# Perceiver layers on one core: in both cross attentions three of four rounds of scores stand later in their half sequence, and the last value projection stands between the turns of tiles 11 and 12

## What is computed

```
def _L1_xattn_ref(query, key, value, mask, Wq, bq, Wk, bk, Wv, bv, Wo, bo):
    q = _split_heads(query @ Wq.T + bq)
    k = _split_heads(key @ Wk.T + bk)
    v = _split_heads(value @ Wv.T + bv)
    scores = jnp.einsum('bhqd,bhkd->bhqk', q, k) / jnp.sqrt(jnp.float32(DEPTH))
    scores = scores + mask * jnp.float32(-1000000000.0)
    weights = jax.nn.softmax(scores, axis=-1)
    ctx = jnp.einsum('bhqk,bhkd->bhqd', weights, v)
    ctx = ctx.transpose(0, 2, 1, 3).reshape(query.shape[0], -1, D_MODEL)
    return ctx @ Wo.T + bo
```

## Time and profile before

| | us |
|---|---|
| median of 3 runs | 2361.56 |
| lowest and highest run | 2360.01, 2362.49 |
| the profiled execution | 2358.21 |
| its span | 2356.4 |
| busy in the span: PE, PE weight loads | 2071.3, 1579.9 |
| busy in the span: DVE, ACT, POOL | 1347.8, 1091.2, 474.8 |

### The profile page before, as it was taken

How to read it: one execution, slowest core, us unless ns; L and a number is a source line. 1 busy time by engine, 2 the same in 40 slices (tenths; PEclk the granted TensorE clock), 3 DMA queues, 4 the chain that set the end, 5 groups by cost and what they waited for, 6 DMA issues and landing times. The chain is left out here.

```text
span 2356.4 us, 60046 instructions
## 1 busy us (share of the span) xinstructions
PE 2071.3 (88%) x25136; PEld 1579.9 (67%) x25136; DVE 1347.8 (57%) x3549; ACT 1091.2 (46%) x2087; POOL 474.8 (20%) x377
## 2 busy tenths in 40 slices
PE   6899999999999985567996899999999999997874
PEld 3677777777777762346994677777777777764453
DVE  4466666666666657834114466666666666663685
ACT  1644545554454543511321455554555554451681
POOL 2311112221111100211002333332223333200010
PEclk9999999999999997787998999999999999996857
DMA  2111111111111001032321311121211112100000
GB/s 87 40 47 30 30 30 30 39 33 45 30 30 30 17 2 54 1 107 99 115 100 47 83 44 53 45 61 44 58 44 44 53 46 61 30 2 21 1 1 25
DMA packets 62413, 103.60 MB, mean 44 GB/s; under 512 B 15417, under 2 KB 30914, under 8 KB 62146
## 3 DMA queue, kind: packets, MB, share of 16 engines
q1 hardware_dynamic: 62146, 99.76, 14.4%
HBM read 98.70 MB, written 1.05 MB: 42 GB/s over the span
## 5 line engine op out<-in xcount | busy, mean ns | idle before, releaser
L628 DVE CUSTOM_DVE_ANT_0 maps_d<-scores_d,mask_scaled_d 128x512 f32<-128x512 f32 (+1 forms) x512 | 263.6, 572 | 212.3 <-PE scores_d L491 205.1
L628 DVE CUSTOM_DVE_ANT_0 maps_a<-scores_a,no_mask_a 128x512 f32<-128x512 f32 (+1 forms) x512 | 263.6, 572 | 208.7 <-PE scores_a L491 208.7
L501 PE MATMUL turn_a<-const,maps_a 128*128 128x128 f32 (+1 forms) x1664 | 259.3, 282 | 21.3 <-DVE mapsT_a L656 15.4
L501 PE MATMUL turn_d<-const,maps_d 128*128 128x128 f32 (+1 forms) x1664 | 259.3, 282 | 21.3 <-DVE mapsT_d L656 15.3
L501 PEld LDWEIGHTS turn_d<-const,maps_d 128*128 128x128 f32 (+1 forms) x1664 | 184.3, 142 | 79.2 <-issue 30.2
L501 PEld LDWEIGHTS turn_a<-const,maps_a 128*128 128x128 f32 (+1 forms) x1664 | 184.2, 142 | 79.2 <-issue 30.2
L580 ACT ACTIVATE mapsT_a<-turn_a 128x512 f32<-128x512 f32 x224 | 129.7, 595 | 230.6 <-PE turn_a L501 230.5
L580 ACT ACTIVATE mapsT_d<-turn_d 128x512 f32<-128x512 f32 x224 | 129.7, 595 | 230.4 <-PE turn_d L501 230.3
L585 ACT ACTIVATE maps_a<-maps_a,neg_max_a 128x1024 f32<-128x1024 f32 (+1 forms) x256 | 222.0, 952 | 1.9 <-DVE neg_max_a L635 1.9
L585 ACT ACTIVATE maps_d<-maps_d,neg_max_d 128x1024 f32<-128x1024 f32 (+1 forms) x256 | 222.0, 952 | 1.9 <-DVE neg_max_d L635 1.9
L284 POOL CAST ctx_hi_a<-raw_a 128x1024 fp32r<-128x1024 f32 x64 | 55.0, 860 | 585.0 <-PE project_a L110 451.1
(11 more groups left out here) (395 smaller groups left out, 4409.0 us busy)
## 6 DMA issues: line engine op xcount, KB each, us to landing
raw_a<-in_ctxT SPq DMA_DIRECT2D x48, 512.0 KB, 3.9
raw_d<-in_ctxT SPq DMA_DIRECT2D x48, 512.0 KB, 3.9
w_c<-in_L_ffn_W SPq DMA_DIRECT2D x23, 1024.0 KB, 5.3
mask_scaled_d<-in_mask SPq DMA_DIRECT2D x32, 400.2 KB, 5.2
raw_a<-in_ctxT SPq DMA_DIRECT2D x16, 65.0 KB, 2.0
raw_d<-in_ctxT SPq DMA_DIRECT2D x16, 65.0 KB, 2.0
x<-in_x SPq DMA_DIRECT2D x1, 1024.0 KB, 5.8
Wk_c_b<-in_L_attn_Wk_c SPq DMA_DIRECT2D x1, 1024.0 KB, 7.0
```

The source lines that it names most:

```text
L501: ins = nc.tensor.transpose(TP[at % 2][0:r, P * j:P * j + P], maps[g % 2][:, j, P * t:P * t + r], chip.ident)
L628: nc.vector.tensor_tensor_reduce(maps[b][:, j, cols], SC[j][:, 0:w], mf[m % 2][:, cols] if masked else none[:, 0:w], 1.0, NEG, ALU.add, AL ...
```

## The change

The second and third round move behind other work of their own tile, the fourth moves from tile 6 to tile 7, and the last value unit of a half sequence moves from tile 12 (even) or tile 9 (odd) to tile 11. In the PE loop, a round at tile 2 (`ROUND_LAST`) now comes behind the values of tiles 0 and 1, and a round at a tile that also has a key unit (tiles 4 and 7) now comes behind that unit. DVE's and ACT's code is as it was; their order follows the tables.

```diff
-V_AT = [{3: 0, 6: 1, 9: 2, 12: 3}, {3: 4, 6: 5, 9: 6}]
-ROUND_AT = {0: 0, 2: 1, 4: 2, 6: 3}
+V_AT = [{3: 0, 6: 1, 9: 2, 11: 3}, {3: 4, 6: 5, 11: 6}]
+ROUND_AT = {0: 0, 2: 1, 4: 2, 7: 3}
+ROUND_LAST = (2,)
...
                     turn(g, t)
-                    if t in ROUND_AT and g + 1 < GROUPS:
+                    if t in ROUND_AT and t not in ROUND_LAST and t not in K_AT and g + 1 < GROUPS:
                         scores(g + 1, ROUND_AT[t])
                     if t in K_AT and m + 1 < NB:
                         k_unit(m + 1, 4 * h + K_AT[t])
+                    if t in ROUND_AT and t in K_AT and g + 1 < GROUPS:
+                        scores(g + 1, ROUND_AT[t])
                     if t in V_AT[h] and m + 1 < NB:
                         v_unit(m + 1, V_AT[h][t])
...
                         values(g, t - 2)
                         values(g, t - 1)
+                    if t in ROUND_LAST and g + 1 < GROUPS:
+                        scores(g + 1, ROUND_AT[t])
```

## The result

The changed kernel takes **2415.38 us** (median of 4 runs, 2413.70 to 2420.52) against 2360.78 us (4 runs) for the kernel before: a ratio of 1.0236 [1.0217, 1.0255], or 54.6 us slower. The forecast was 2427 us in a range of 2396 to 2455, from a sum of +65. The profiled execution was the slowest of the four, 2420.52 us with a span of 2418.7.

The account below looks back on a forecast made before the run. PE's list sets the time, through its waits and order. Odd half sequences 1.00 and even ones 1.29 slower give 66.2, with -1 for the ends +65; from 2358.2 profiled to 2423.4, plus 3.4 for the median: 2427 us, range 2396 to 2455.

Parts of the forecast that it names:

- Up to tile 3: Second round of scores starts at 4.65 without the 0.43 wait; tile 3 starts 0.52 earlier.
- Tile 4: k1 must wait for v0's keep on ACT and starts at 8.58, losing 0.53.
- rival of a quick keep: The keep ahead of k1 is quicker than taken, so no loss there: 31 us less, 2396; 6%.
- Tiles 4 to 9: PE is 0.10 ahead at tile 9; DVE's `negate` comes at 18.11 instead of 14.18; ACT's `exp` still costs nothing.
- The value unit stands in the backlog: At tile 11 the last value unit waits 1.34 us for k3's keep, behind DVE's `finish` and move of tile 10.
- the value unit fills the wait: Rival: k3's keep is done by 21.86, the unit starts at once, saving 38 us: 2324; 6%.
- The odd half sequence: An odd half sequence takes 25.82 us, 1.00 slower than 24.82; 15 per attention.
- the move of tile 10 1.96 later: On DVE, the move of tile 10 starts 1.96 after `finish`, at 22.17, with k3's keep following at 22.77 to 23.05.
- the end after the turn of tile 12: In odd half sequences the turn of tile 12 starts at 23.98, its values at 25.46, the next half sequence at 25.82.
- the even half sequence: v3 starts at 24.54 and no longer covers tile 12's move; the half sequence is 1.29 slower than 26.65.
- The clock: No fall expected from waits of 1.34 and 1.0 us; the rival of a fall adds 51 us, 2478; 6%.
- The last but one half sequence: It has no projections and waits for DVE's rounds; the later fourth round was to gain about 1.3 us.

Follow-up runs that it names:

- Experiment 8: The kernel before with only the second round moved behind the values of tiles 0 and 1: 2351.83 us, 0.9958.
- Experiment 3: The changed kernel with the values of tiles 2 and 3 put ahead of k1 at tile 4: 2387.79 us, 1.0112.
- Experiment 2: The kernel before with only the last value unit moved to tile 11: 2402.64 us, 1.0176.
- experiment 10: `order_only` with `finish` split (tiles 8 and 2), values ahead of k3, last value unit at tile 11: 2311.52 us; without that unit's move 2275.32.
- Experiment 4: The changed kernel with the sums and DVE's `finish` at tile 12 instead of 9: 2399.85 us, 1.0162.
- `order_only`: The kernel before with second and fourth rounds behind their tile's values, and at tile 4 values, k1, then third round: 2317.46 us, 0.9808.

## Why the prediction was right, and where it was off

- **What bounds the kernel.** Right: PE's list and its waits. The stretches of the two attentions grew by 55.1 us, with PE's busy time by 15.0.
- **Up to tile 3.** Right: the second round started at 4.66 without idle (forecast 4.65). Experiment 8 shows its worth alone, 10.7 us.
- **Tile 4.** k1 started at 8.59 (forecast 8.58), with 0.34 idle in the record. From start to start that is a loss of 0.53, just what was forecast. The 0.15 from the end of a keep to the next product, for which the prediction shows no row, measured 0.14 here (425.93 to 426.07) and 0.15 at tile 11. Experiment 3 prices this wait: 27.6 us, where the rival of a quick keep had 31. That rival did not happen.
- **Tiles 4 to 9.** The turn of tile 9 started at 18.38 (forecast 18.45), `negate` at 18.05 (18.11), the reciprocal at 20.12 (20.21). `exp` cost nothing, as forecast, with 0.98 of cover where 1.3 was forecast.
- **The value unit stands in the backlog.** Right as to what ends its wait: in the odd half sequence k3's keep ended at 22.86 and not by 21.86, with DVE busy all the way from `negate`, so the rival ("the value unit fills the wait") fell. The wait was 1.17 from start to start (440.49 less 438.91 less 0.41) where 1.34 was forecast; the record shows 0.93 of it as idle, where "about 1.3" was to be seen, and 0.66 in even half sequences where 1.0 was. Experiment 2 gives the unit's place 41 of the 55 us. Too narrow is the thought that it is all the backlog: experiment 10 has the same place cost 36 us without one.
- **The size was high by 10 us in the sum** (65 against 54.6; the forecast of 2427 was 11.6 above the measured time). The odd half sequence was 0.34 shorter than forecast. The term that was mis-sized is the step "the move of tile 10 1.96 later": it measured 1.86 (437.60 to 439.46). The 1.96 held a last instruction of `finish` of 0.37, beside which POOL was at work (0.44 us from 426.06); in the changed kernel, where POOL does that work later, it is 0.28 in all 64 half sequences. With 0.09 from the earlier reciprocal this brings the unit forward by 0.19. The unit itself took 0.73 (440.49 to 441.22), not 0.78, and the end after the turn of tile 12 took 1.38 (441.22 to 442.60), not 1.48. In the even half sequence the unit came forward by 0.19 too, but the values of tile 12 started 1.63 behind their turn and not 1.53, which leaves 0.10.
- **The clock.** No fall: the waits of 0.93 and 0.66 us left it at 1.00, and so did waits of 1.15 and 1.71 us in the last but one half sequence, where the kernel before had 1.83 us and a fall. Experiment 4, with 2.30 us of wait, did show one. The fall in each step of a loop of which the Trainium skill tells ("TensorE: Matmul & The Clock Gate", section "HAM oscillation — how this bites in real kernels") did not come about in the changed kernel.
- **The last but one half sequence** gained 1.6 us (21.36 to 19.74) where 1.3 was forecast; before, its clock was 0.92 on the mean, now 1.00.
- **Small errors without harm to the number.** An even half sequence has a wait ahead of the second round too (0.42), which the prediction's list of waits leaves out and its sum does not. And 2358.2 + 65 is 2423.2, not 2423.4.
- **What the prediction did not look for** is the state with the fourth round at tile 6, in which DVE has gaps that PE ends. It shows in `order_only`, which gained 20 us more than I expected.

Left open: whether another bank for the last value unit would make its place good, and what moving `finish` gives the kernel before by itself. Neither was run.

## What to carry to other kernels

Before a piece of work is put into a wait, look at what that piece itself waits for: if its input, or here its one output bank, comes from behind the same backlog, it fills nothing and everything behind it moves back. Shorten the backlog (split the long step and put its parts where the engine has gaps), and place the work where both the copy ahead of it and its own copy have cover; the first without the second still cost 36 us here. When an instruction moves in time, list what every other engine does at the new time.

## What the hardware showed that I had not expected

- A VectorE product of 128 x 128 with both inputs in SBUF took 0.29 us alone and 2.76 us where GpSimd had started a 4.27 us multiplication in SBUF 0.65 us before it. GpSimd's own time did not change (4.27 either way). A copy out of PSUM beside another GpSimd instruction kept its time (0.69 at 423.45 in the kernel before, beside a split from 423.05 to 425.25).
- The time of such a collision was lost on PE, which takes no part in it: as a wait for scores of 2.30 us, and then as a lower granted clock.
- Between a keep out of the bank and PE's next product into it lay 0.15 us. A turn of 0.41 us between two units that share the bank was too little cover for the keep of even a small unit (0.29 us): 0.23 us was lost.
